# The routed gate product moved from VectorE to ScalarE and POOL in an attention and mixture-of-experts kernel

## Chip, cores and metric

One core of one Trainium2 chip. The metric is the device time of one execution in microseconds (us); three executions of the kernel before took 546.87, 548.35 and 548.81 us.

## What is computed

The input x has shape (4, 1024, 128). It is normalised over its last axis; xn goes to two branches, an attention and a mixture of experts, and the result is x + attention(xn) * silu(ffn(xn)). The expert branch, cut to what matters here (sixteen experts of inner size 64, four chosen per token, and a shared expert of inner size 128):

```python
hg = jnp.einsum('nh,eih->nei', xf, Wg)
hu = jnp.einsum('nh,eih->nei', xf, Wu)
act = jax.nn.silu(hg) * hu
y = jnp.einsum('nei,ne,ehi->nh', act, cw, Wd)          # cw: routing weight, 0 for experts not chosen
shared = jax.nn.silu(xf @ Ws_g.T) * (xf @ Ws_u.T) @ Ws_d.T
```

The attention has 16 heads of dimension 8, four over all earlier tokens and twelve over a window of 32.

## The kernel before

**Tiling.** Everything is kept transposed, with features on partitions and tokens on the free axis. A batch (1024 tokens) is two chunks of 512 columns. Two experts of inner size 64 fill 128 partitions, so a chunk has eight tiles t = 0 to 7 of two routed experts and a ninth, t = 8, for the shared expert: NUP = 9 tiles, EP = 8 of them routed, 72 in all over four batches and two chunks. All experts are computed for all tokens, and the routing weight, spread over the partitions of its expert by a matmul with pairsel (L749), multiplies the hidden values.

**One expert tile.** The silu is written as a product with 1 + tanh(g/2). The step ("up", c, t) makes up to three PSUM tiles on PE: the routing weight (L749), the gate product g and the up product u, each of the last two from three matmuls (L544 to L546). Then:

- ScalarE, step up: hid = tanh(0.5 g) (L828), and, for a routed tile, wrow = the routing row (L834).
- VectorE, step up: hid = (hid + 1) * g (L1121), which frees the gate's bank.
- VectorE, step times: hid = hid * u (through the helper tt, L933), which frees the up product's bank.
- POOL (GpSimd), step times, routed tiles only: hid = hid * wrow (L1243).
- PE, step down: the down projection accumulates in bank Y (L765). For a routed tile it waits for POOL, for the shared expert for VectorE.

hid has NHID = 5 buffers and wrow NWT = 3. PSUM's eight banks are a ring of three for the attention, a ring of three for the expert products and other preparations, one accumulator for the attention and one (Y) for the experts.

**The order of the work.** There is no scheduler at run time. Streams of steps are woven by strings written out by hand, one letter per step: R attention scores and products with the values, A making a head group's operands (strips, which is two DMAs from a plane in HBM, pads and kpads, which are the copies at L1065 and L1077, max, which is the row maxima at L1165 and L1167, maxdone, L1234, and qfull), X expert steps, P preparing the next batch, T its routing, V its values, C and 0 and 1 the context and output. FIRST_ORDER is the start, BODY_ORDER is a batch with the next batch's preparation woven in (three times), LAST_ORDER is the last batch. Every engine walks the same list of steps in this order and executes its own part of each, so an instruction that waits holds back everything later in the list on its engine, and only there.

Within the X stream the steps of a chunk follow each other so:

```python
for t in range(NUP + LAG_DOWN):          # LAG_DOWN = 3
    if 1 <= t <= NUP:
        out.append(("times", c, t - 1))
    if t < NUP:
        out.append(("up", c, t))
    if t >= LAG_DOWN:
        out.append(("down", c, t - LAG_DOWN))
```

The first six tiles of chunk 0 of a batch are computed in the section before it (SPLIT).

**Around it.** VectorE also makes the padded 16-bit operands by copies of 32 x 1024 elements within SBUF (L1065, L1077), the row maxima from PSUM, the routing (some forty small passes over 128 x 128 tiles in SBUF, mostly through L933), the layer norm and the reciprocals of the softmax sums (L1106). ScalarE evicts the scores through exp (L905) and the other PSUM tiles. POOL makes the diagonal of maxima (L1234), the low parts of x, q and k, and the context and output products.

## Time and profile before

| | |
|---|---|
| median of three runs | 548.35 us |
| profiled execution, own time | 548.62 us |
| its span | 546.8 us |
| PE busy | 482.4 us, 88% of the span |
| VectorE (DVE) busy | 435.4 us, 80%, 939 instructions |
| ScalarE (ACT) busy | 298.1 us, 55%, 582 instructions |
| POOL busy | 179.9 us, 33%, 167 instructions |
| mean granted TensorE clock | 0.982 of full speed |

The span is the stretch that the profiler's instruction records cover, and the execution's own time stands 1.8 us above it. Busy time counts an engine's instructions only, not its waits. PE is the matmul engine, PEld its weight loads, which overlap the matmuls. In a group of instructions, the idle time is that of the engine just before them, and the name behind it is what ended it. The chain of waits follows the work back from the last instruction, at each step to what released it or to the instruction before it on its engine.

### The profile page before, as it was taken

The page shows a single profiled execution, that of the slowest core. Times are in us where ns is not written, and L with a number is a line of the kernel's source. Part 1 is how long each engine was busy: PE and PEld are TensorE (multiplying, and loading weights), DVE is VectorE, ACT ScalarE, POOL GpSimd, SP SyncE. Part 2 cuts the span into 40 slices and gives each one's busy share as a digit, 9 for nine tenths or more (in the row PEclk, how much of TensorE's full clock was granted, in tenths as well). Part 3 has the DMA queues.
Part 4 walks back from the last instruction along what each step waited for, and adds up shares of the span by engine and source line. Part 5 has one row for each costly group of instructions (what it writes and reads, how often), then busy time and mean ns, then how long its engine had stood idle before and what let it go on. Part 6 is the DMA issues. An engine that isn't in the chain of part 4 may idle for free.

```text
span 546.8 us, 10352 instructions
## 1 busy us (share of the span) xinstructions
PE 482.4 (88%) x3832; PEld 286.5 (52%) x3832; DVE 435.4 (80%) x939; ACT 298.1 (55%) x582; POOL 179.9 (33%) x167
## 2 busy tenths in 40 slices
PE   1758978999999987999998997899999989989994
PEld 1546655555445754545445764545445656644442
DVE  6888798885998799876899789887799768788524
ACT  3524743656945453665955444564975445564862
POOL 3504621123524541113522633104341633103302
PEclk9969998999999999999999999999999999999997
DMA  8270210000310421000130331000040041000001
GB/s 209 87 222 0 79 40 1 2 2 1 115 40 2 115 78 41 2 1 0 54 102 1 91 104 40 1 2 1 1 155 1 26 130 40 2 0 2 1 0 38
DMA packets 26571, 25.00 MB, mean 46 GB/s; under 512 B 3462, under 2 KB 18842, under 8 KB 26522
## 3 DMA queue, kind: packets, MB, share of 16 engines
q1 hardware_dynamic: 26192, 24.06, 14.6%
q8 instruction: 30, 0.49, 0.4%
q10 hardware_dynamic: 330, 0.30, 0.3%
q14 instruction: 19, 0.16, 0.1%
HBM read 14.91 MB, written 9.44 MB: 45 GB/s over the span
## 4 chain that ended last, share of the span: by engine, by line
PE 43%; DVE 38%; issue 6%; ACT 4%; DVEq 4%; DMA 4%; POOL 1%; SPq 0%; POOLq 0%; ACTq 0%
PE bank L765 6%; DVE kpad L1077 5%; DVE qpad L1065 5%; PE bank L648 5%; DVE mxp L1167 5%; DVE denT L1106 4%; PE bank L544 4%; PE bank L546 3%; PE bank L545 3%; PE bank L725 3%; DVE mxp L1165 3%; DVE hid L933 3%; PE bank L709 3%; DMA kall<-planes 3%; PE bank L678 3%
## 5 line engine op out<-in xcount | busy, mean ns | idle before, releaser
L905 ACT ACTIVATE stage<-bank 128x512 f32<-128x512 f32 (+3 forms) x240 | 112.5, 519 | 68.6 <-PE bank L682 41.3
L1243 POOL TENSOR_TENSOR hid<-hid,wrow 128x512 f32<-128x512 f32 x64 | 82.6, 1293 | 150.6 <-DVE hid L933 150.5
L1165 DVE TENSOR_REDUCE mxp<-bank 128x1 f32<-128x512 f32 (+4 forms) x192 | 89.8, 518 | 13.6 <-PE bank L648 6.8
L1121 DVE SCALAR_TENSOR_TENSOR hid<-hid,bank 128x512 f32<-128x512 f32 x72 | 49.0, 680 | 40.7 <-ACT hid L828 40.5
L1234 POOL TENSOR_TENSOR maxd<-mxp,k 128x512 f16<-128x512 f32 x32 | 36.5, 1140 | 126.7 <-DVE mxp L1167 81.6
L765 PE MATMUL bank<-hid,down_w 128*128 128x512 f32 x144 | 76.0, 615 | 0.0
L828 ACT ACTIVATE hid<-bank 128x512 f32<-128x512 f32 x72 | 43.2, 600 | 45.7 <-PE bank L546 45.0
L544 PE MATMUL bank<-xh,up_hi 128*128 128x512 f32 x144 | 59.5, 413 | 4.7 <-DVE hid L933 3.1
L648 PE MATMUL bank<-kall,qpad 128*128 128x512 f16 (+4 forms) x192 | 50.1, 318 | 9.0 <-DVE mxp L1165 3.9
L546 PE MATMUL bank<-xl,up_hi 128*128 128x512 f32 x144 | 56.7, 394 | 0.0
L545 PE MATMUL bank<-xh,up_lo 128*128 128x512 f32 x144 | 56.5, 392 | 0.0
L678 PE MATMUL bank<-kpad,kall 128*128 128x512 f16 (+3 forms) x192 | 54.8, 330 | 1.6 <-ACT stage L905 0.9
L933 DVE TENSOR_TENSOR hid<-hid,bank 128x512 f32<-128x512 f32 x72 | 49.0, 680 | 1.3
L678 PEld LDWEIGHTS bank<-kpad,kall 128*128 128x128 f16 x192 | 17.4, 97 | 48.8 <-issue 31.1
L1065 DVE COPY qpad<-qtmp 32x1024 f16<-32x1024 f16 x64 | 35.5, 555 | 6.1 <-DMA kall<-planes 5.5
L709 PE MATMUL bank<-stage,vg 128*32 128x512 f32 (+3 forms) x384 | 40.0, 497 | 0.0
L834 ACT ACTIVATE wrow<-bank 128x512 f32<-128x512 f32 x64 | 38.2, 597 | 3.2 <-PE bank L749 3.2
L648 PEld LDWEIGHTS bank<-kall,qpad 128*128 128x128 f16 x192 | 17.3, 97 | 34.9 <-DVE mxp L1165 17.1
L898 ACT ACTIVATE qall<-bank 128x512 f16<-128x512 f32 x32 | 18.8, 597 | 28.7 <-PE bank L635 28.3
L544 PEld LDWEIGHTS bank<-xh,up_hi 128*128 128x128 f32 x144 | 27.2, 189 | 12.9 <-DVE hid L933 5.3
L1167 DVE TENSOR_REDUCE mxp<-bank 128x8 f32<-128x512 f32 x48 | 31.2, 685 | 2.5 <-PE bank L660 2.1
L749 PE MATMUL bank<-cwT,pairsel 128*128 128x512 f32 x64 | 32.9, 514 | 0.0
(158 smaller groups left out, 908.0 us busy)
## 6 DMA issues: line engine op xcount, KB each, us to landing
planes<-qkh SPq DMA_DIRECT2D x16, 256.0 KB, 3.5
qtmp<-planes SPq DMA_DIRECT2D x16, 256.0 KB, 2.6
kall<-planes SPq DMA_DIRECT2D x16, 256.0 KB, 3.0
xin<-in_L_attn_x_dram SPq DMA_DIRECT2D x4, 512.0 KB, 4.5
planes<-qkl SPq DMA_DIRECT2D x8, 256.0 KB, 3.5
xres<-in_L_attn_x_dram SPq DMA_DIRECT2D x4, 512.0 KB, 4.1
...
```

The source lines that it names most:

```text
L544: pe.matmul(ps[:], w_hi, x_hi, start=True, stop=False)
L545: pe.matmul(ps[:], w_lo, x_hi, start=False, stop=False)
L546: return pe.matmul(ps[:], w_hi, x_lo, start=False, stop=True)
L648: ins = pe.matmul(ps[:, 0:cols], qpad[:, j, :, :], kall[:, g % 2, CH * c:CH * c + cols], start=True, stop=not last, skip_group_check=True)
L678: ins = pe.matmul(ps[:, 0:cols], kall[:, g % 2, P * j:P * (j + 1)], kpad[:, g % 2, q0 // BLK:(q0 + cols) // BLK, h, :], start=True, stop=n ...
L765: pe.matmul(banks[Y][:], down_w[:, t, :], hid[:, i % NHID, :], start=(t == 0), stop=(t == NUP - 1)).then_inc(down_done, 1)
L905: act.activation(prob[:, t % NPROB, 0:cols], ps[:, 0:cols], ACT.Exp).then_inc(freed, 1)
L933: return dve.tensor_tensor(out_, a, b_, op)
L1065: ins = dve.tensor_copy(qpad[r, :, h, :], qtmp[r, g % 2, :].rearrange("p (j q) -> p j q", q=BLK))
L1165: ins = dve.tensor_reduce(mxp[:, c, j:j + 1], ps[:, 0:cols], AX_X, ALU.max)
L1167: ins = dve.tensor_reduce(mxp[:, 0, LOC * n:LOC * (n + 1)], ps[:].rearrange("p (j q) -> p j q", q=2 * BLK), AX_X, ALU.max)
L1243: pool.tensor_tensor(hid[:, i % NHID, :], hid[:, i % NHID, :], wrow[:, iw % NWT, :], ALU.mult)\
```

## The change

The product is taken in another grouping: before, ((tanh + 1) * g) * u * w, after, ((tanh + 1) * u) * (g * w). ScalarE copies the gate product from PSUM into a new SBUF tile, gates (one buffer), which frees the gate's bank. POOL multiplies the routing row in place with gates (step up, routed tiles), with a new semaphore, gated. VectorE makes one pass, hid = (hid + 1) * u (step times). POOL multiplies hid with that row, or, for the shared expert, with gates. PE's step down waits for POOL in every tile. Before filling gates for tile t, ScalarE waits for POOL's gating of tile t - 1, and for t = 0 for the shared expert's last multiplication of the chunk before. The three orders are woven anew.

```diff
--- before.py
+++ after.py
@@ -144,14 +144,14 @@
     return out
 
 
-FIRST_ORDER = ("PIPPIIPPPPITTPPPTTTPITTIIITIPIVIPIPPPPIPTPVXVXVXXIVXXVXXXIVXVXXVVXXX")
-BODY_ORDER = ("PAAXARXRXARRXAAAARARRRRAAAXAXAAPXRAARXRARARAAXXRRAAAAAAAAAARPRAAAXAAAXAARXAAAXXRRRARXAARARAARAAA"
-              "AARRRARAAARRRARAARAAXARRRXRARRAPAARXRRRARRXRAAARAXRRAXRRAXRRRAARAAPRRRPAARXRRXXRXRRRRRPRTPRRXRRR"
-              "RRPPTRRRXTRRTXXRRRRXCRRRCRPRRRRXXRRRRRRTXXPRXRTRRRRRRXPPPRRRRRPRRXRRRXRXRRTRXRRRXPRTTRP0CXCXV0PX"
-              "XVXX01VXVX1XX1VXXVXVVVVXX")
-LAST_ORDER = ("AXARARAXRXAAAAAAAAXRAAARRRRAAARAXRXRAAXXARXRAAAARRAAAAARARAAAXAAAXAAAXARARRRRRAXRRAAAARAAAXAARRX"
-              "RRAXRARRAAXRRRRAAAARAAARARAARARAAAXAARXRAXARAXRAARRXRXRRRRRRRRRRRAAXRRXRXRXRRXRRCRRRXCRRRRRRRRXR"
-              "RRRRRRRXXRRRRRRRRRRRRRRRXRRRRRRRRXRRRXRRRRRRXRRRRRRXRR0X0XCCXXXX0111")
+FIRST_ORDER = ("IPIIPPIPIPVTPIPPPPPTTTTITTIIVTVTIIVIXPXVIPPPXXPIXXVXXXVPPPXVXXVIVXXX")
+BODY_ORDER = ("PAAAXRXXARRRRXAARRAAAAARARXXAAAXPARAAARRRRAARAAXAAAXAARPAAARAAAXAAAXAAAXARRRRXAXAXRXAARRAAARRRAA"
+              "AAARARRAAARRRARARAAAXRARRXRARAPAARRXRARRRRRXAAARAXARRXXRARRRRAARRAAPRRPARXACRRXRXXRRRXRPRRTPRRRR"
+              "RRTPPRXRPRRRRXRXRXRRRRRTTXRRXXTRRRRRRTTXRXXRXRRRRRRPRCPRRRXRRPPRRRRRRRPXRRXRXRRRRRPTTRPCXCXV00XV"
+              "X11XVVV0XVXXVX1VXVPXXXVXX")
+LAST_ORDER = ("AAARRRXXAXAAAXRRAAARRRAAARXAAAAAXAAAXRXRARRAAAARRARAAAAAXRAAAXAAAXAAAXARRRARRAXRARRAAARAAAXAARRX"
+              "AAXRRRRARARRARRXAARAAAARARAARARAXAAARXARAAXARAAXRRRRRRXRRRRRRRRRAXAXRRXXRRXRXRRRRRRRRRRRRRXCXRRR"
+              "RRCRXRRRRRRRRRRXRRRRXRRRRRRRRRXRRRRRRRRRRXRXRRRRRRRRRXX0X0CCXXXX0111")
 
 
 FIRST_EXPERTS = expert_steps(0) + [("z", 0), ("z2", 0)]
@@ -389,6 +389,7 @@
         hid = sb("hid", [P, NHID, CH])
         wqk = hid[:, 0, 0:2 * D]
         wrow = sb("wrow", [P, NWT, CH])
+        gates = sb("gates", [P, CH])
         tz = sb("tz", [P, CH])
 
         filled = [sem(f"bank{i}_filled") for i in range(BANKS)]
@@ -431,6 +432,7 @@
         ctx_ready = sem("ctx_ready")
         hid_ready = sem("hid_ready")
         tanh_ready = sem("tanh_ready")
+        gated = sem("gated")
         o_ready = sem("o_ready")
         stored = [sem(f"stored{c}") for c in range(NCH)]
 
@@ -757,11 +759,7 @@
                         i = NUP * c + t
                         if t == 0:
                             fill(at, ("y", c))
-                        if t < EP:
-                            pe.wait_ge(hid_ready, of * NCH * EP + (EP * c + t + 1))
-                        else:
-                            up = ("up", c, t, "up")
-                            pe.wait_ge(emptied[at.bank(up)], at.taken(up))
+                        pe.wait_ge(hid_ready, of * NCH * NUP + (i + 1))
                         pe.matmul(banks[Y][:], down_w[:, t, :], hid[:, i % NHID, :],
                                   start=(t == 0), stop=(t == NUP - 1)).then_inc(down_done, 1)
                     elif kind == "outT":
@@ -826,11 +824,16 @@
                             act.wait_ge(down_done, of * NCH * NUP + (i - NHID + 1))
 
                         act.activation(hid[:, i % NHID, :], banks[at.bank(gate)][:], ACT.Tanh, scale=0.5).then_inc(tanh_ready, 1)
+                        if t > 0:
+                            act.wait_ge(gated, of * NCH * EP + (EP * c + t))
+                        elif of or c:
+                            act.wait_ge(hid_ready, of * NCH * NUP + NUP * c)
+                        act.activation(gates[:], banks[at.bank(gate)][:], ACT.Copy).then_inc(emptied[at.bank(gate)], 1)
                         if t < EP:
                             iw = EP * c + t
                             act.wait_ge(filled[at.bank(weight)], at.filled(weight))
                             if iw >= NWT:
-                                act.wait_ge(hid_ready, of * NCH * EP + (iw - NWT + 1))
+                                act.wait_ge(hid_ready, of * NCH * NUP + (NUP * ((iw - NWT) // EP) + (iw - NWT) % EP + 1))
                             act.activation(wrow[:, iw % NWT, :], banks[at.bank(weight)][:], ACT.Copy)\
                                 .then_inc(emptied[at.bank(weight)], 1)
                         continue
@@ -1114,20 +1117,14 @@
                         dve.wait_ge(tz_ready, at.of(s) * NCH + (c + 1))
                         dve.scalar_tensor_tensor(out=z[:, chunk(c)], in0=tz[:], scalar=1.0, in1=z[:, chunk(c)],
                                                  op0=ALU.add, op1=ALU.mult).then_inc(z2_ready, 1)
-                    elif kind == "up":
-                        i = NUP * s[1] + s[2]
-                        gate = s + ("gate",)
-                        dve.wait_ge(tanh_ready, at.of(s) * NCH * NUP + (i + 1))
-                        dve.scalar_tensor_tensor(out=hid[:, i % NHID, :], in0=hid[:, i % NHID, :], scalar=1.0,
-                                                 in1=banks[at.bank(gate)][:], op0=ALU.add, op1=ALU.mult)\
-                            .then_inc(emptied[at.bank(gate)], 1)
                     elif kind == "times":
                         c, t = s[1], s[2]
                         i = NUP * c + t
-                        gate, up = ("up", c, t, "gate"), ("up", c, t, "up")
-                        dve.wait_ge(emptied[at.bank(gate)], at.taken(gate))
+                        up = ("up", c, t, "up")
+                        dve.wait_ge(tanh_ready, at.of(s) * NCH * NUP + (i + 1))
                         dve.wait_ge(filled[at.bank(up)], at.filled(up))
-                        tt(hid[:, i % NHID, :], hid[:, i % NHID, :], banks[at.bank(up)][:], ALU.mult)\
+                        dve.scalar_tensor_tensor(out=hid[:, i % NHID, :], in0=hid[:, i % NHID, :], scalar=1.0,
+                                                 in1=banks[at.bank(up)][:], op0=ALU.add, op1=ALU.mult)\
                             .then_inc(emptied[at.bank(up)], 1)
                     elif kind == "weights" and s[1] == 2:
                         continue
@@ -1234,13 +1231,22 @@
                         pool.tensor_tensor(maxd[:, blocks, :], mxp[:, 0, blocks].unsqueeze(2).broadcast_to([P, BPC, BLK]),
                                            const32("eye32").unsqueeze(1).broadcast_to([P, BPC, BLK]), ALU.mult)\
                             .then_inc(maxd_ready, 1)
-                    elif kind == "times" and s[2] < EP:
+                    elif kind == "up" and s[2] < EP:
+                        gate, weight = s + ("gate",), s + ("weight",)
+                        row = wrow[:, (EP * s[1] + s[2]) % NWT, :]
+                        pool.wait_ge(emptied[at.bank(gate)], at.taken(gate))
+                        pool.wait_ge(emptied[at.bank(weight)], at.taken(weight))
+                        pool.tensor_tensor(row, row, gates[:], ALU.mult).then_inc(gated, 1)
+                    elif kind == "times":
                         c, t = s[1], s[2]
-                        up, weight = ("up", c, t, "up"), ("up", c, t, "weight")
-                        i, iw = NUP * c + t, EP * c + t
-                        pool.wait_ge(emptied[at.bank(weight)], at.taken(weight))
+                        gate, up = ("up", c, t, "gate"), ("up", c, t, "up")
+                        i = NUP * c + t
+                        pool.wait_ge(emptied[at.bank(gate)], at.taken(gate))
                         pool.wait_ge(emptied[at.bank(up)], at.taken(up))
-                        pool.tensor_tensor(hid[:, i % NHID, :], hid[:, i % NHID, :], wrow[:, iw % NWT, :], ALU.mult)\
+                        if t < EP:
+                            pool.wait_ge(gated, at.of(s) * NCH * EP + (EP * c + t + 1))
+                        pool.tensor_tensor(hid[:, i % NHID, :], hid[:, i % NHID, :],
+                                           wrow[:, (EP * c + t) % NWT, :] if t < EP else gates[:], ALU.mult)\
                             .then_inc(hid_ready, 1)
                     elif kind == "ctx":
                         q = CH * s[1] + QTR * s[2]
```

## Rows read from the trace of the kernel before

**Rows 1.** The page's table of busy time by engine.

```profile
PE 482.4 (88%) x3832; PEld 286.5 (52%) x3832; DVE 435.4 (80%) x939; ACT 298.1 (55%) x582; POOL 179.9 (33%) x167
```

**Rows 2.** Windows by batch: length; busy PE, PEld, DVE, ACT, POOL; clock, DMA.

```profile
0.00:62.90 62.90, 39.75 (x200) 30.49 (x201) 51.03 (x136) 27.42 (x49) 23.15 (x34) 0.92 0.41 113
...
190.90:317.00 126.10, 117.10 (x952) 69.00 (x951) 107.13 (x231) 71.88 (x142) 43.87 (x38) 1.00 0.14 43
...
443.50:546.80 103.30, 89.69 (x784) 48.01 (x782) 65.92 (x119) 55.32 (x111) 24.89 (x23) 0.97 0.07 21
```

**Rows 3.** The page's chain of waits, shares by engine.

```profile
PE 43%; DVE 38%; issue 6%; ACT 4%; DVEq 4%; DMA 4%; POOL 1%; SPq 0%; POOLq 0%; ACTq 0%
```

**Rows 4.** Windows through the second body, columns as in rows 2.

```profile
190.90:227.00 36.10, 31.36 (x399) 19.83 (x397) 33.74 (x77) 18.14 (x33) 10.37 (x9) 1.00 0.14 45
...
254.00:281.10 27.10, 26.94 (x126) 13.57 (x126) 20.72 (x53) 22.55 (x43) 11.80 (x11) 1.00 0.25 78
281.10:299.00 17.90, 16.07 (x126) 8.46 (x124) 16.58 (x29) 9.55 (x23) 3.25 (x4) 1.00 0.01 1
299.00:317.00 18.00, 17.48 (x79) 12.66 (x80) 14.02 (x30) 7.20 (x15) 11.52 (x10) 1.00 0.30 87
```

**Rows 5.** Groups by line: operations of an expert tile (busy, mean, idle before).

```profile
L1243 POOL TENSOR_TENSOR hid<-hid,wrow 128x512 f32<-128x512 f32 x64 | 82.6, 1293 | 150.6 <-DVE hid L933 150.5
...
L1121 DVE SCALAR_TENSOR_TENSOR hid<-hid,bank 128x512 f32<-128x512 f32 x72 | 49.0, 680 | 40.7 <-ACT hid L828 40.5
L933 DVE TENSOR_TENSOR hid<-hid,bank 128x512 f32<-128x512 f32 x72 | 49.0, 680 | 1.3
```

**Rows 6.** DVE's timeline: the instruction after an L1121 pass.

```profile
208.22 0.68 DVE L1121 SCALAR_TENSOR_TENSOR hid<-hid,bank 128x512 f32<-128x512 f32 x1
208.82 1.28 DVE L1167 TENSOR_REDUCE mxp<-bank 128x8 f32<-128x512 f32 x2
```

**Rows 7.** The 16-bit copies: groups by line, then shortest, median and longest.

```profile
L1065 DVE COPY qpad<-qtmp 32x1024 f16<-32x1024 f16 x64 | 35.5, 555 | 6.1 <-DMA kall<-planes 5.5
...
L1077 DVE COPY kpad<-kall 32x1024 f16<-32x1024 f16 x48 | 29.2, 608 | 0.5
...
L1065 DVE COPY qpad<-qtmp x64: 405/420/1420, 37.6 to 466.7; 32x1024 f16<-32x1024 f16 x64
...
L1077 DVE COPY kpad<-kall x48: 404/423/1178, 41.6 to 461.8; 32x1024 f16<-32x1024 f16 x48
```

**Rows 8.** Small routing passes: groups, then DVE's and POOL's timelines.

```profile
L933 DVE TENSOR_TENSOR cmp<-cmp 128x128 f32<-128x128 f32 x8 | 6.6, 825 | 0.6
...
L933 DVE TENSOR_TENSOR msk<-msk,gm 128x128 f32<-128x128 f32 x4 | 3.9, 978 | 0.3
...
L933 DVE TENSOR_TENSOR eq<-msk,top 128x128 f32<-128x128 f32 x4 | 3.3, 821 | 0.0
L933 DVE TENSOR_TENSOR cmp<-cmp,k 128x128 f32<-128x128 f32 x4 | 3.2, 793 | 0.3
...
264.48 1.17 DVE L933 TENSOR_TENSOR cmp<-cmp 128x128 f32<-128x128 f32 x1
...
267.38 0.29 DVE L933 TENSOR_TENSOR cmp<-cmp 128x128 f32<-128x128 f32 x1
...
264.34 1.16 POOL L1224 TENSOR_TENSOR qkl<-sT,qkh 128x512 f16<-128x512 f32 x1 [3.46 <-ACT qkh L893]
```

**Rows 9.** ScalarE's timeline: a tanh and the row copy behind it.

```profile
271.09 0.64 ACT L828 ACTIVATE hid<-bank 128x512 f32<-128x512 f32 x1
271.57 0.66 ACT L834 ACTIVATE wrow<-bank 128x512 f32<-128x512 f32 x1
```

**Rows 10.** Timelines of POOL and ScalarE, then the chain, before a body's end.

```profile
302.10 1.06 POOL L1234 TENSOR_TENSOR maxd<-mxp,k 128x512 f16<-128x512 f32 x1
...
315.99 1.09 ACT L898 ACTIVATE qall<-bank 128x512 f16<-128x512 f32 x2 [2.87 <-PE bank L635]
...
317.05 4.29 DMA kall<-planes
```

## The prediction

> **What bounds the kernel now.** I read the page's table of busy times first [rows 1]. TensorE is busy 88% of the span and VectorE 80%; ScalarE (55%) and POOL (33%) have room. The windows by batch then show that the kernel is a start of 62.9 us, three bodies of some 126 us and a last batch of 103.3 us, and that in a body PE is busy 117.10 and DVE 107.13 of 126.10 us [rows 2]. The end of a matmul is modelled in this trace, so a busy PE need not be a full one. The chain of waits says how the two share the limit: 43% of the chain is PE, 38% DVE, 4% ACT, 1% POOL [rows 3]. Inside a body the bound changes [rows 4]: in the first 36.1 us (maxima and paddings of the local heads) DVE is busy 33.74 us, in the middle (254.0 to 281.1) PE is busy 26.94 of 27.10 and DVE 20.72, from 281.1 to 299.0 DVE again with 16.58 of 17.90, and in the last 18 us (six expert tiles packed together) PE with 17.48, while POOL, idle elsewhere, is busy 11.52. The groups of lines give the price of an expert tile [rows 5]: two DVE passes of 680 ns (L1121 and the hid group of L933), a POOL pass of 1293 ns. DVE also stands idle 40.7 us in front of L1121, waiting for the tanh.
>
> **DVE, removed.** 72 passes go, one per tile. In a full DVE queue the next instruction starts 0.60 us after such a pass (208.22, then 208.82 [rows 6]), so the pass costs 0.60 us of queue, not 0.68: 72 x 0.60 = 43.2 us. The idle time in front of L1121 shrinks too, since the one pass that is left stands where the second stood, steps behind the tanh. I count that at nothing: it lies mostly where PE is the fuller engine, and PE's work covers it.
>
> **POOL, added.** A gating pass for each of 64 tiles, and a pass for the 8 shared-expert tiles that had none: 72 x 1.293 = 93.1 us on 179.9. Their own room is there; their neighbour is the question. The four copies into the padded operands have medians of 420 and 423 ns but means of 555 and 608, with a maximum of 1420 [rows 7]. The excess, 64 x 0.135 + 48 x 0.185 = 17.5 us, falls on copies beside a POOL pass. The routing's small passes show the same [rows 8]: a 128x128 cmp takes 0.29 us at 267.38, with POOL at rest, and 1.17 us at 264.48, with a POOL pass running since 264.34. By that 0.29, the groups cmp, msk, eq and cmp with the constant hold 8 x 0.535 + 4 x (0.688 + 0.531 + 0.503) = 11.2 us more. Together 28.7 us of DVE time for 167 POOL instructions, 0.17 us each. For 72 more passes I take the same mean: 72 x 0.172 = 12.4 us given back to DVE. The bounds are nothing (every new pass beside a DVE pass that reads PSUM) and 72 x 1.0 us, the longest excess of a copy (1.42 less 0.42).
>
> The Trainium skill (SBUF — State Buffer, Who interferes with whom) says that GpSimd and a DVE instruction with two SBUF inputs or in a two-port mode exclude each other for a whole instruction, whoever issues second waiting; by it all 72 passes could each stop DVE for their full length, and DVE's queue would grow. Direction and kind of victim agree with the rows; how often it happens is the rows' to say.
>
> **Sum on DVE.** 43.2 - 12.4 = 30.8 us, 7.1% of its 435.4 us. DVE's part of the chain is 0.38 x 546.8 = 207.8 us; shrunk alike, it gives **-14.7 us**.
>
> **ACT, added.** 72 copies of the gate product. A copy right behind another ACT pass costs its start-to-start 0.48 us (271.09, then 271.57 [rows 9]): 34.6 us, 11.6% of 298.1. On ACT's 4% of the chain (21.9 us) that is **+2.5 us**. The copy also frees the gate's bank, which until now waited for DVE's first pass; PE was seldom held by it, so nothing is counted.
>
> **POOL's part of the chain.** 1% is 5.5 us; 51.7% more work there is **+2.8 us**.
>
> **The added waits.** There is one gates buffer. ACT may fill it for tile t+1 only after POOL's gating of tile t, and on POOL that gating stands behind the final multiplication of tile t-1, which waits for DVE. Behind ACT's wait stand the row copy of the same tile and every exp and eviction after it. A tight loop is gate copy, row copy, gating: 0.48 + 0.66 + 1.29 = 2.4 us [rows 5, 9], and POOL's two passes are 2.6 us a tile. The packed stretch now takes 18.0 us for six tiles, 3.0 each, so it fits, barely. PE's multiplication for the shared expert now waits for POOL instead of DVE, 1.29 us later, eight times; the two steps of lag behind it cover that.
>
> **The orders.** The three interleavings move many steps within one pattern; the number of every kind of instruction stays, the DMAs included (strips issue two each, q and k three each). In the body, the strips of head group 0 go ahead of six exp steps, two parts of the routing and an expert tile, on SP past nothing else; their data are wanted later than now, so I count nothing. In the start, a memset of the padded keys goes ahead of the statistics and three weight tiles go ahead of most of the routing: DVE has 11.9 us idle there [rows 2], so this could give or take a few us. I count nothing, and the range has room for it. The late maximum of group 0 (maxdone) moves behind three more tiles on POOL. Today that pass starts at 302.10, while the ACT pass that depends on it runs at 315.99 [rows 10], and the strips of group 1, on the chain at 317.05 as the DMA into kall, wait for that. Those 13 us cover a move; if the cover is gone, each of three bodies starts up to two POOL passes late, 3 x 2.6 = 7.8 us. What is late next, when DVE is shorter, is PE.
>
> **Total.** -14.7 + 2.5 + 2.8 = -9.4 us, from the profiled execution's 548.62 us (a span of 546.8 and 1.8 around it) to 539.2. That execution stands 0.3 us above the median of the three runs, 548.35, so the number is **539.0 us**.
>
> **Rivals.**
> 1. *The bound is PE, and DVE's relief only makes DVE idle.* For it: PE's 117.10 of 126.10 us, against DVE's 107.13 [rows 2]; a body could gain at most those 9 us of PE idle time. Against: 38% of the chain. Then only the start, with six tiles, gains 6 x 0.60 x 0.38 = 1.4 us: 547 us. Chance 0.18.
> 2. *The larger gain.* The new POOL passes meet no copies and the handoffs are hidden: 43.2 / 435.4 x 207.8 = 20.6 us, 528 us. For it: the heaviest copying lies outside the packed expert tiles. Against: the collisions now, and PE's small room. Chance 0.17.
> 3. *Slower: POOL passes hold DVE at the paddings and the routing.* In the DVE-bound stretch the passes for tiles 6 to 8 run beside 16-bit copies that already grow from 0.42 to 1.42 us. Break-even is where DVE's saving, times 207.8/435.4, equals the 5.3 us of the other engines: 43.2 - 72e = 11.1, e = 0.45 us per added pass; today's mean is 0.17, the worst 1.0. At 0.72, DVE grows by 8.6 us, the chain by 4.1, with the 5.3 9.4 us: 558 us; at 1.0 it is 568. Chance 0.15. The page named above is this rival's rule: at 1.29 us a pass DVE grows by 49.9 us, and the time would be 578.
>
> The forecast itself, 534 to 545 us, has 0.50. The 80% range is 528 to 552 us: it takes in rival 1, half of rival 2 down to its full value, and rival 3 up to just under its middle. A measurement can tell about 0.5% from no change, 2.7 us. Faster by more: 0.50 + 0.17 = 0.67; within: 0.18; slower: 0.15.
>
> **What would show it.** In the profile of the changed kernel: DVE busy near 400 us, with 72 fewer passes; ACT near 335, POOL near 273. The means of the copies at L1065 and L1077 tell the collisions: near 0.65 us for the forecast, near 0.58 as now for rival 2, 0.85 or more for rival 3. DVE's share of the chain should fall and PE's rise; body lengths should be 123 to 124.5 us. Waits of the ACT gate copy for POOL above some 10 us in total would speak for the single buffer as the price I underrated; bodies of 126 us with DVE idle behind PE would speak for rival 1. The prediction is wrong in kind if the copies keep their means and the time still does not fall.

## The result, and the profile after

The change made the kernel slower: 580.66 us (median of four runs, 580.32 to 582.14) against 548.53 for the kernel before beside it, a ratio of 1.060 with a 95% interval of 1.057 to 1.064. The forecast was 539.0 us, the range ended at 552. The profiled execution took 580.32 us, its span is 578.5.

The page's table of busy times, its row of the granted clock over 40 slices, and the chain's shares by engine (they answer to [rows 1] and [rows 3]; the clock's row is in tenths of full speed):

```profile
PE 491.5 (85%) x3832; PEld 289.9 (50%) x3832; DVE 428.7 (74%) x867; ACT 331.1 (57%) x654; POOL 272.4 (47%) x239
...
PEclk9869998898989999999997999889998999999999
...
PE 42%; DVE 36%; ACT 7%; issue 7%; DVEq 4%; DMA 2%; POOL 1%; SPq 0%; POOLq 0%; ACTq 0%
```

The 72 DVE passes are gone (939 instructions became 867), 43.2 us of queue at the 0.60 us from start to start of [rows 6], yet DVE's busy time fell by 6.7 us only: what is left grew by 36.5 us. PE ran the same 3832 instructions and was busy 9.1 us longer. The groups of lines say which passes grew (they answer to [rows 5] and [rows 7]; the new line L1239 is the gating pass):

```profile
L1248 POOL TENSOR_TENSOR hid<-hid,wrow 128x512 f32<-128x512 f32 x64 | 83.3, 1302 | 16.8 <-DVE hid L1126 9.9 <-POOL wrow L1239 6.8 <-DVE mxp L1164 0.2
L1239 POOL TENSOR_TENSOR wrow<-wrow,gates 128x512 f32<-128x512 f32 x64 | 82.8, 1294 | 105.5 <-ACT wrow L837 105.3
...
L1126 DVE SCALAR_TENSOR_TENSOR hid<-hid,bank 128x512 f32<-128x512 f32 x72 | 48.7, 677 | 39.4 <-ACT hid L826 19.8 <-PE bank L548 19.1
L1068 DVE COPY qpad<-qtmp 32x1024 f16<-32x1024 f16 x64 | 45.1, 705 | 9.7 <-DMA kall<-planes 8.9
L831 ACT ACTIVATE gates<-bank 128x512 f32<-128x512 f32 x72 | 42.9, 596 | 3.9 <-POOL wrow L1239 3.9
L1080 DVE COPY kpad<-kall 32x1024 f16<-32x1024 f16 x48 | 33.5, 699 | 0.6
```

The pass that is left, with one input in SBUF and one in PSUM, is as long as before (677 ns against 680). The copies within SBUF went from 555 to 705 and from 608 to 699 ns, 14 us together, and the third kind (L1087, L1084 before) adds 2.8. Most of the rest lies in small passes within SBUF for the routing and the layer norm: eight over 128 x 64 elements (pm from sfc) went from 1.5 to 6.4 us in total, four that make sc from 0.9 to 3.9. ScalarE's copy waited for POOL 3.9 us in all, so little speaks for the single buffer as the price (no run changes it).

The windows by batch (columns as in [rows 2], with boundaries at the next batch's first layer-norm statistics), start, three bodies, last batch:

```profile
0.00:62.45 62.45, 37.97 (x195) 28.67 (x196) 49.01 (x124) 29.07 (x53) 27.19 (x32) 0.89 0.41 113
62.45:201.96 139.51, 122.40 (x951) 71.77 (x950) 107.00 (x213) 80.42 (x160) 67.91 (x61) 0.95 0.12 37
201.96:336.38 134.42, 119.43 (x952) 70.14 (x950) 105.32 (x213) 80.03 (x159) 67.06 (x56) 0.97 0.13 40
336.38:474.30 137.92, 121.38 (x954) 70.85 (x951) 105.98 (x213) 80.66 (x161) 68.07 (x57) 0.96 0.12 38
474.30:578.50 104.20, 90.29 (x786) 48.49 (x786) 61.36 (x107) 60.87 (x123) 42.20 (x36) 0.99 0.07 21
```

With the same boundaries the kernel before has 61.80, 127.83, 126.10, 126.44 and 104.63 us. All of the loss is in the bodies: 11.7, 8.3 and 11.5 us. The windows of the second body, cut at four events, say where. Stretch 1 runs from the statistics to the first copy of L1084 (L1087 after), which is the local heads with the paddings; stretch 2 to the tanh of the router's scores; stretch 3 is the routing, up to the pass that writes cw; stretch 4 runs to the next statistics and ends with most of the packed tiles. The kernel before:

```profile
189.63:227.89 38.26, 33.52 (x429) 21.49 (x428) 35.01 (x84) 19.98 (x35) 12.21 (x10) 1.00 0.13 43
227.89:254.64 26.75, 24.97 (x213) 14.25 (x207) 22.07 (x45) 13.61 (x30) 6.78 (x7) 1.00 0.01 1
254.64:290.06 35.42, 34.43 (x192) 16.58 (x196) 29.12 (x70) 25.74 (x53) 13.59 (x12) 1.00 0.19 61
290.06:315.73 25.67, 24.18 (x134) 16.69 (x131) 20.93 (x34) 12.55 (x24) 11.29 (x10) 1.00 0.21 61
```

And the kernel after:

```profile
201.96:242.47 40.51, 33.76 (x441) 22.15 (x438) 36.18 (x80) 21.20 (x39) 17.80 (x15) 1.00 0.15 47
242.47:270.03 27.56, 24.64 (x200) 13.93 (x197) 21.78 (x42) 15.04 (x32) 12.16 (x11) 1.00 0.01 2
270.03:300.77 30.74, 29.16 (x136) 13.87 (x134) 21.55 (x52) 25.82 (x51) 16.64 (x14) 1.00 0.22 69
300.77:336.38 35.61, 31.86 (x182) 20.19 (x183) 25.81 (x39) 17.96 (x38) 20.45 (x18) 0.90 0.13 37
```

Stretch 1 has four DVE passes fewer and DVE is busier, 36.18 against 35.01 us: the saving is given back within it. Stretch 4 has a clock of 0.90, where before has 1.00. Stretches 3 and 4 can only be compared as a sum, 66.4 against 61.1 us, since the new orders move PE's work over the boundary (x192 and x134 became x136 and x182). The orders thus had to be taken apart from the instructions first.

### The profile page after: what moved, and what is told of

Its sections match the earlier page's. It is cut to its first block, busy times and chain, and to the rows that moved or that the text cites. A ratio compares the mean times of both kernels' runs of the same rounds, so it can differ in the third digit from the quotient of the medians.

```text
span 578.5 us, 10499 instructions
## 1 busy us (share of the span) xinstructions
PE 491.5 (85%) x3832; PEld 289.9 (50%) x3832; DVE 428.7 (74%) x867; ACT 331.1 (57%) x654; POOL 272.4 (47%) x239
## 4 chain that ended last, share of the span: by engine, by line
PE 42%; DVE 36%; ACT 7%; issue 7%; DVEq 4%; DMA 2%; POOL 1%; SPq 0%; POOLq 0%; ACTq 0%
DVE qpad L1068 6%; PE bank L763 6%; PE bank L650 5%; DVE kpad L1080 5%; DVE mxp L1164 4%; DVE mxp L1162 4%; PE bank L546 4%; PE bank L548 3%; PE bank L547 3%; PE bank L711 3%; PE bank L680 3%; DMA kall<-planes 2%; DVE hid L1126 2%; ACT stage L908 2%; DVE xin L939 2%
## 5 line engine op out<-in xcount | busy, mean ns | idle before, releaser
L908 ACT ACTIVATE stage<-bank 128x512 f32<-128x512 f32 (+3 forms) x240 | 112.4, 523 | 78.2 <-PE bank L684 46.6
L1239 POOL TENSOR_TENSOR wrow<-wrow,gates 128x512 f32<-128x512 f32 x64 | 82.8, 1294 | 105.5 <-ACT wrow L837 105.3
L763 PE MATMUL bank<-hid,down_w 128*128 128x512 f32 x144 | 79.4, 640 | 0.0
L1231 POOL TENSOR_TENSOR maxd<-mxp,k 128x512 f16<-128x512 f32 x32 | 36.6, 1142 | 84.3 <-DVE mxp L1164 49.0
L650 PE MATMUL bank<-kall,qpad 128*128 128x512 f16 (+4 forms) x192 | 52.8, 331 | 13.6 <-DVE mxp L1162 10.3
L680 PE MATMUL bank<-kpad,kall 128*128 128x512 f16 (+3 forms) x192 | 58.2, 343 | 1.1 <-DVE mxp L1162 0.6
L1068 DVE COPY qpad<-qtmp 32x1024 f16<-32x1024 f16 x64 | 45.1, 705 | 9.7 <-DMA kall<-planes 8.9
L831 ACT ACTIVATE gates<-bank 128x512 f32<-128x512 f32 x72 | 42.9, 596 | 3.9 <-POOL wrow L1239 3.9
L711 PE MATMUL bank<-stage,vg 128*32 128x512 f32 (+3 forms) x384 | 41.1, 509 | 0.0
L656 PE MATMUL bank<-kbf 128*128 128x512 bf16 x48 | 19.4, 404 | 21.9 <-DVE qpad L1068 21.9
```

The costliest lines, as they stand in the source:

```text
L650: ins = pe.matmul(ps[:, 0:cols], qpad[:, j, :, :], kall[:, g % 2, CH * c:CH * c + cols], start=True, stop=not last, skip_group_check=True)
L680: ins = pe.matmul(ps[:, 0:cols], kall[:, g % 2, P * j:P * (j + 1)], kpad[:, g % 2, q0 // BLK:(q0 + cols) // BLK, h, :], start=True, stop=n ...
L763: pe.matmul(banks[Y][:], down_w[:, t, :], hid[:, i % NHID, :], start=(t == 0), stop=(t == NUP - 1)).then_inc(down_done, 1)
L908: act.activation(prob[:, t % NPROB, 0:cols], ps[:, 0:cols], ACT.Exp).then_inc(freed, 1)
L1068: ins = dve.tensor_copy(qpad[r, :, h, :], qtmp[r, g % 2, :].rearrange("p (j q) -> p j q", q=BLK))
L1239: pool.tensor_tensor(row, row, gates[:], ALU.mult).then_inc(gated, 1)
```

## The experiments

Three theories. **A: POOL's passes hold DVE** by traffic in SBUF (the prediction's third rival). **B: POOL's queue.** The passes of the experts stand ahead of others that PE waits for, the maxima's above all (L1231, before L1234), whoever else is at work. **C: the orders**, which I had counted as nothing, or the added waits.

### Instructions and orders apart

e1_old_orders has the instructions of after in the orders of before, e2_new_orders the reverse.

```diff
 e1_old_orders, on the kernel after:
-BODY_ORDER = ("PAAAXRXXARRRRXAARR...
+BODY_ORDER = ("PAAXARXRXARRXAAAAR...
 e2_new_orders, on the kernel before:
-BODY_ORDER = ("PAAXARXRXARRXAAAAR...
+BODY_ORDER = ("PAAAXRXXARRRRXAARR...
 (FIRST_ORDER and LAST_ORDER likewise)
```

> The changed kernel's instructions, woven in the three orders of the kernel before. Theory P (the 72 added POOL passes cost: they stop DVE's SBUF copies and routing passes, and they pace the packed expert tiles): the time stays near the changed kernel's, 575 to 590 us, with DVE's copies still at means of 0.65 us or more. Theory O (the new orders are what lost the time, by work put late): back to 540 to 552 us. Theory W (the single gates buffer and the longer chain from POOL to ScalarE): 570 to 590 us too, but with the ScalarE gate copy waiting for POOL for 20 us or more in total.

> The kernel before's instructions, woven in the new orders. Theory P: the orders are nearly neutral, 545 to 556 us. Theory O: most of the 32 us comes with the orders alone, 570 us or more. Theory W says the same as P here: 545 to 556 us.

e1: 583.51 us, ratio 1.064 (1.060 to 1.068). e2: 583.4 us, 1.065 (1.062 to 1.068). Two things follow. The instructions alone cost 35 us. And the new orders are far from neutral: on the old work they cost 35 us as well (DVE waits 80.0 us for the tanh where it waited 40.5, and PE 18.8 us for the paddings where it waited 5.1), and on the new work they neither cost nor bring more than 3 us. They belong to the new instructions, and neither order makes those fast. Everything below that asks for the mechanism can use the old orders, where the stretches hold the same work. The windows of e1's second body by stretch, then stretch 1 of its third body:

```profile
202.36:244.58 42.22, 33.48 (x429) 21.46 (x428) 34.89 (x80) 21.73 (x39) 17.86 (x14) 1.00 0.13 39
244.58:271.38 26.80, 24.92 (x213) 14.15 (x207) 20.40 (x42) 15.00 (x32) 10.15 (x9) 1.00 0.01 2
271.38:306.78 35.40, 34.57 (x196) 16.70 (x196) 30.75 (x65) 27.82 (x58) 20.23 (x17) 1.00 0.19 60
306.78:334.84 28.06, 24.90 (x130) 16.37 (x123) 17.35 (x28) 15.39 (x30) 18.78 (x16) 1.00 0.20 55
334.84:382.05 47.21, 37.82 (x429) 24.65 (x428) 34.92 (x80) 21.74 (x39) 17.84 (x14) 0.89 0.12 36
```

Against before: +4.0, +0.1, 0.0, +2.4 us. In the two middle stretches PE is busy 93 to 98% of the time, and DVE's busy time is 1.7 us less in one and 1.6 us more in the other without effect. Stretch 1 loses though DVE is busy no more than before, and the second body is the mildest: in the first and the third, with the same instructions, stretch 1 takes 47.8 and 47.2 us, both at a clock of 0.89. I come back to that. PE's waits for the maxima's pass of POOL are 20.1 us in all of e1, 8.1 before; in after they are 7.0, but there PE waits 21.9 us for the paddings, 5.1 before (9.9 in e1). So the two orders pay at different places. In stretch 4 POOL, with two passes of 1.29 us a tile and its others, is the one that the packed tiles wait for.

### Is it the added passes?

e3_short_gating takes the kernel after and lets the gating pass work on 32 of 512 columns.

```diff
-pool.tensor_tensor(row, row, gates[:], ALU.mult).then_inc(gated, 1)
+pool.tensor_tensor(row[:, 0:32], row[:, 0:32], gates[:, 0:32], ALU.mult).then_inc(gated, 1)
```

> The changed kernel with POOL's gating pass cut to 32 of 512 columns, every wait and semaphore kept; the routing row is multiplied with the gate product in those columns only, so the output lacks the gate factor in the rest. Theory P: the gating passes' own length is the cost; with 64 of the 72 added passes shortened from 1.29 to some 0.2 us the time falls below the kernel before, 530 to 550 us. Theory W: the waits stay, so most of the loss stays, 565 us or more. Theory O: also 565 us or more.

560.1 us, 1.021 (1.019 to 1.024): 20.6 us less than after. POOL is busy 66.2 us less and DVE 26.2 us less (402.5). Every instruction and wait of the change is there, so two thirds of the loss is the length of the 64 gating passes. I had expected 530 to 550 us if it were all of it: 12 us over the kernel before are left, and no run divides them among ScalarE's copies, the shared expert's passes and the orders.

e4_before_plus_passes goes the other way: the kernel before, with 64 POOL passes on which nothing depends. They stand where the gating stands; they read one column of a constant, broadcast, and write 128 x 512.

```diff
+elif kind == "up" and s[2] < EP:
+    pool.wait_ge(emptied[at.bank(weight)], at.taken(weight))
+    held = half[:, 0:1].broadcast_to([P, CH])
+    pool.wait_ge(idled, at.of(s) * NCH * EP + EP * s[1] + s[2])
+    pool.tensor_tensor(idle_out[:], held, held, ALU.mult).then_inc(idled, 1)
 (idle_out and idled are a new tile and a new semaphore)
```

> The kernel before, its own orders, with one POOL pass of 128x512 fp32 added for each of the 64 routed tiles at the step up; it reads and writes tiles that nobody else uses, so nobody waits for its result, it only takes POOL's time and its way to SBUF. Theory P: DVE loses some 0.5 us or more a pass as in the changed kernel, and has not lost the 72 passes of its own: 575 to 600 us. Theory W or O: nothing depends on the passes and POOL has room, 547 to 553 us.

578.31 us, 1.052 (1.047 to 1.057). Nothing waits for these passes, no DVE pass is removed, and the time is 30 us longer. The page's busy times and the group of the passes:

```profile
PE 494.7 (86%) x3832; PEld 295.6 (51%) x3832; DVE 447.8 (78%) x939; ACT 298.8 (52%) x582; POOL 244.8 (42%) x231
...
L1244 POOL TENSOR_TENSOR idle_out<-half 128x512 f32<-128x512 f32 x64 | 67.4, 1053 | 119.7 <-ACT wrow L836 119.5
```

DVE grew by 12.4 us, exactly what the forecast had given back to it (0.19 us a pass here, 0.17 there). By the forecast's own rates that is 12.4 x 207.8/435.4 + 67.4/179.9 x 5.5 = 8 us. It cost 30. This run judges the pricing alone, apart from how many collisions there are.

e5_passes_off_sbuf keeps the passes and takes the traffic away: a power on 5 columns, which lasts as long.

```diff
-pool.tensor_tensor(idle_out[:], held, held, ALU.mult).then_inc(idled, 1)
+pool.tensor_tensor(idle_out[:, 0:5], idle_out[:, 8:13], half[:, 0:5], ALU.pow).then_inc(idled, 1)
 (and a memset of idle_out at the start)
```

> The kernel before with 64 added POOL instructions as in e4, at the same steps and behind the same wait, but each a pow over 5 columns: about as long, with next to no traffic to SBUF. Theory P1 (the added passes cost by shutting VectorE's copies and two-input passes out of SBUF): back to 548 to 556 us. Theory P2 (they cost by holding POOL's queue, by their length and by their wait, so that its other passes come late): stays at 568 to 580 us. In between, both.

566.87 us, 1.033 (1.030 to 1.036). Its passes have a mean of 1177 ns, 12% longer than e4's, and DVE's busy time is 436.5 us, 1.1 above before. So 18 us come nearly without collisions, by occupying POOL's queue (B) and what the clock adds to it, and the other 12 of e4's 30 by traffic (A); since e5's passes are longer, that is traffic's least share. Neither theory alone stands. The trace of e5 has the queue at work, and the clock beside it. For 28 us the second body's stretch 1 keeps PE's times of the kernel before. Then a phase at the lower clock (0.57 in the window 222 to 226) puts it 1.6 us behind, though PE's instructions and waits up to there were the same. Then the last maxima's pass starts at 232.78, directly behind an added pass, and PE stands idle 1.43 us before the matmul that needs it (at 233.93; in the kernel before 0.13 us, at 226.63): that is the queue's 1.3 us. By stretches of the second body, stretch 3, with the routing's small passes, takes 39.2 us in e4 and 35.4 in e5, as before; stretch 1 takes 43.2 and 41.1, stretch 4 27.3 and 29.4. This division is rough, because the clock falls in other places in other bodies: in the first and third body of e5 stretch 3 takes 36.9 and 37.1 us, and its stretch 4 takes 29.4 at a clock of 0.94 and 27.7 in the first body at 1.00.

e9_wait_only leaves e4's wait and drops the pass.

```diff
 pool.wait_ge(emptied[at.bank(weight)], at.taken(weight))
-held = half[:, 0:1].broadcast_to([P, CH])
-pool.wait_ge(idled, at.of(s) * NCH * EP + EP * s[1] + s[2])
-pool.tensor_tensor(idle_out[:], held, held, ALU.mult).then_inc(idled, 1)
```

> The kernel before with POOL's wait for ScalarE's row copy at the step up (64 times), as in e4 and e5, and no pass behind it. e5 left 18 us that are not traffic: if the wait's place is that cost (it holds the maxima's passes that stand behind it), 558 to 567 us; if the length of the passes is, 548 to 551 us.

548.6 us, 1.000 (0.998 to 1.003). The wait costs nothing; the occupation does. Two more runs move the gating pass from the step up to the step times, so that POOL never stands waiting for it ahead of others: e10_late_gating_old_orders on e1, e11_late_gating on after.

```diff
-elif kind == "up" and s[2] < EP:
-    ...
-    pool.tensor_tensor(row, row, gates[:], ALU.mult).then_inc(gated, 1)
 elif kind == "times":
     ...
+    if t < EP:
+        pool.tensor_tensor(row, row, gates[:], ALU.mult).then_inc(gated, 1)
```

> e1 (the changed kernel's instructions in the old orders, 583.5 us) with POOL's gating pass moved from the step up to the step times, right ahead of the final multiplication, so that its wait for ScalarE no longer stands ahead of the maxima. If the held queue costs: 565 to 576 us. If the passes' length and traffic cost: 580 to 586 us.

> The changed kernel in its own orders with the same move of the gating pass. The new orders already put the maxima's pass of head group 3 ahead of the first tile of chunk 1, so the hold should be small here: 576 to 582 us. Below 573 us would say that the hold is the price in these orders too; above 584 us that the pass is better done early.

583.44 us, 1.063 (1.058 to 1.068), as e1; and 586.38 us, 1.069 (1.065 to 1.073), 6 us above after: there the pass is better done early. The theory that POOL's early wait holds its queue fell with these and e9.

### Where the passes hurt

e6_packed_passes has e4's passes only for the six packed tiles of each batch (24), e7_other_passes only for the others (40).

```diff
 e6_packed_passes:
-elif kind == "up" and s[2] < EP:
+elif kind == "up" and s[1] == 0 and s[2] < SPLIT_PAIR:
 e7_other_passes:
-elif kind == "up" and s[2] < EP:
+elif kind == "up" and s[2] < EP and not (s[1] == 0 and s[2] < SPLIT_PAIR):
 (the count of idled in the wait likewise)
```

> As e4, with the added passes only at the six tiles of each batch that are packed together (24 of the 64). P1: the copies next to them are the only ones hit, 552 to 558 us. P2, POOL pacing the packed tiles: 560 to 568 us, a body's last stretch some 3 to 4 us longer. If neither: 548 to 551 us.

> As e4, with the added passes only at the other ten routed tiles of each batch (40 of the 64). P1: 560 to 570 us, since the paddings of the local heads stand beside them. P2: 555 to 565 us, by the maxima's pass held behind the wait of the added pass. With e6 it should add up to e4's 30 us; a sum well below that would speak for a cost that needs both, as POOL's backlog running into the paddings.

555.27 us, 1.012 (1.009 to 1.015), and 567.58 us, 1.035 (1.032 to 1.038): 6 and 19 us, 25 together against e4's 30. Per pass 0.3 and 0.5 us. In the second body of e7 stretch 1 grows by 5.1 us and stretch 3 by 3.8 (in the first body by 1.9 and 2.2): the places with copies, maxima and routing are the dearer ones.

e12_shared_only isolates one place: the kernel before with the change for the 8 shared-expert tiles only. Each of these loses a DVE pass and gains a ScalarE copy and a POOL pass, which was not there before.

```diff
 DVE, step up:
+if s[2] == EP:
+    continue
 POOL:
+elif kind == "times" and s[2] == EP:
+    ...
+    pool.tensor_tensor(hid[:, i % NHID, :], hid[:, i % NHID, :], gates[:], ALU.mult).then_inc(hid_ready, 1)
 (ScalarE's copy, DVE's step times and PE's wait for these tiles as in the change)
```

> The kernel before, its own orders, with the change made for the shared expert's tiles only (8 of 72: ScalarE copies the gate, VectorE makes one pass, POOL multiplies by the gate, no gating pass). By the prediction's way of counting, 1 to 2 us faster than the kernel before. By the changed kernel's mean price for a tile (32 us over 72) 3 to 4 us slower. If only the gating pass makes the trouble, within 1.5 us of the kernel before or faster.

557.63 us, 1.016 (1.013 to 1.020). Eight passes cost 9 us, more than one each, and far more than any of my three expectations. Stretch 1 of its second body grew from 38.3 to 41.5 us; in the first and the third body it grew by 0.8 and 3.7 us. These three make up 7.7 us, as much as the profiled execution's span grew (554.5 against 546.8); the other stretches of the second body kept their length within 0.3. The timelines of DVE, POOL and PE there (start, length, instruction, and in brackets the idle time before it):

```profile
213.62 0.69 DVE L1134 SCALAR_TENSOR_TENSOR hid<-hid,bank 128x512 f32<-128x512 f32 x1
214.22 3.44 DVE L1066 COPY qpad<-qtmp 32x1024 f16<-32x1024 f16 x4
...
214.45 1.30 POOL L1253 TENSOR_TENSOR hid<-hid,gates 128x512 f32<-128x512 f32 x1 [3.33 <-DVE hid L1134]
215.72 1.22 POOL L1244 TENSOR_TENSOR maxd<-mxp,k 128x512 f16<-128x512 f32 x1
...
217.00 0.61 PE L635 MATMUL bank<-qtmp,k 128*128 128x512 f16 x1 [2.89 <-POOL maxd L1244]
```

The same instructions in the kernel before, timelines of DVE, POOL and PE:

```profile
214.44 2.06 DVE L1065 COPY qpad<-qtmp 32x1024 f16<-32x1024 f16 x4
...
213.88 1.05 POOL L1234 TENSOR_TENSOR maxd<-mxp,k 128x512 f16<-128x512 f32 x1 [2.55 <-DVE mxp L1167]
...
214.98 0.39 PE L634 MATMUL bank<-qtmp,k 128*128 128x512 f16 x1 [0.66 <-POOL maxd L1234]
```

Read it line by line. DVE's pass on hid ends and releases POOL, so POOL's pass starts beside DVE's next instructions, of necessity. Those are the four padding copies, 3.44 us beside this pass and the next, in place of 2.06 beside the maxima's pass alone. Behind that POOL pass stands the maxima's pass, which before ran first and now starts 1.8 us later. PE, which needs it, waits 2.89 us in place of 0.66. And its next matmul takes 0.61 us in place of 0.39. The windows of e12, the wait, the 7 us behind it, and the next 7, say why (the clock is the third figure from the end):

```profile
214.00:217.00 3.00, 0.11 (x2) 0.01 (x1) 2.97 (x4) 0.60 (x1) 2.49 (x2) 0.96 0.00 0
217.00:224.00 7.00, 6.44 (x58) 4.22 (x58) 3.75 (x14) 2.94 (x5) 0.00 (x0) 0.53 0.01 2
224.00:231.00 7.00, 6.73 (x64) 3.91 (x61) 6.51 (x12) 3.85 (x7) 1.50 (x2) 1.00 0.00 1
```

PE stood idle for 2.9 us, and the granted clock was 0.53 for the next 7 us, nearly all at the lower of the two levels (1.2 GHz), before it was back at full. Of the 3.3 us that this stretch 1 grew by, 2.4 are PE's busy time (35.90 us for the work that took 33.52). One DVE pass traded for one POOL pass thus cost collision, queue and clock at once. That PE's idle time is what lowers the clock is stated by the Trainium skill (TensorE: Matmul & The Clock Gate, HAM oscillation — how this bites in real kernels), and this row agrees in direction; that the length of a wait alone does not decide it is shown in the last section.

e14_shared_moved tests this scene: e12 with the shared tile's step times moved by a few steps, so that the maxima's pass and the copies are issued first.

```diff
+def moved(steps, step, behind):
+    steps.remove(step)
+    steps.insert(steps.index(behind) + 1, step)
+    return steps
 ...
-return woven(LAST_ORDER, streams)
+return moved(woven(LAST_ORDER, streams), ("times", 0, 8), ("pads", 3))
 (BODY_ORDER likewise)
```

> e12 (the change for the shared expert alone, 557.6 us) with one step of the orders moved in the bodies and the last batch: the product with the up tile of the shared expert of chunk 0 stands behind the padding of head group 3 instead of ahead of the second half of group 2's maxima. POOL's new pass then no longer stands ahead of the maxima's pass that PE waits for, and no longer runs beside the padding's copies. If these two are the price that e12 paid: 546 to 551 us. If the price is elsewhere (ScalarE's copy, the down projection's wait for POOL): 555 us or more.

548.3 us, 0.999 (0.997 to 1.001): all 9 us are back, by one step. The timelines of POOL and DVE:

```profile
212.45 1.27 POOL L1250 TENSOR_TENSOR maxd<-mxp,k 128x512 f16<-128x512 f32 x1 [2.55 <-DVE mxp L1183]
215.73 1.27 POOL L1259 TENSOR_TENSOR hid<-hid,gates 128x512 f32<-128x512 f32 x1 [2.01 <-DVE hid L1140]
...
212.40 2.47 DVE L1072 COPY qpad<-qtmp 32x1024 f16<-32x1024 f16 x4
214.90 0.69 DVE L1140 SCALAR_TENSOR_TENSOR hid<-hid,bank 128x512 f32<-128x512 f32 x1
215.50 1.05 DVE L1181 TENSOR_REDUCE mxp<-bank 128x1 f32<-128x32 f32 x5
```

The pass on hid now has row maxima behind it, which read PSUM: they take 1.05 us beside a POOL pass, against 1.06 without one. The eight DVE passes saved bring nothing, though. e18_before_moved is the control, the same move in the kernel before.

> Control of e14: the kernel before with that one step moved and nothing else. If the move is neutral here: 547 to 550 us, and e14's equality with the kernel before means that the change for the shared expert is worth nothing. Below 546 us would mean that the move itself gains and that the change costs what it gains.

548.49 us, 1.001 (0.999 to 1.003). The move has no value of its own; it only takes away what the change had put there. e16_old_orders_moved is e1, the change on all the tiles, with the same move.

> e1 (the whole change in the old orders, 583.5 us) with the one step moved as in e14. The same two troubles lie in it, but four other POOL passes stand in the same stretch (two tiles, two passes each) and POOL paces the packed tiles. If e14's 9 us is there to be had: 573 to 577 us. If the other passes hold the maxima and the paddings anyway: 580 us or more.

574.91 us, 1.050 (1.044 to 1.056), 8.6 us below e1: about as much comes back as in e14, and 27 us of loss are left. One of a batch's 18 tiles is mended, the others are not.

### The relief by itself

e17_short_dve_pass asks what DVE's relief is worth when nothing is added: the kernel before, with L1121 on 32 of 512 columns.

```diff
-dve.scalar_tensor_tensor(out=hid[:, i % NHID, :], in0=hid[:, i % NHID, :], scalar=1.0,
-                         in1=banks[at.bank(gate)][:], op0=ALU.add, op1=ALU.mult)
+dve.scalar_tensor_tensor(out=hid[:, i % NHID, 0:32], in0=hid[:, i % NHID, 0:32], scalar=1.0,
+                         in1=banks[at.bank(gate)][:, 0:32], op0=ALU.add, op1=ALU.mult)
```

> The kernel before with VectorE's first pass of each tile (L1121, the one that the change removes) cut to 32 of 512 columns, every wait kept and nothing added anywhere: the worth of the relief by itself. The factor 1 + tanh times the gate is left out in the other columns. The prediction's sum (DVE's saving times DVE's share of the chain) says some 36 us of DVE queue, 17 us of time: 529 to 534 us. If PE holds the time wherever DVE is relieved: 543 to 549 us.

542.87 us against 547.93, 0.990 (0.986 to 0.994). The chain's shares, and the four stretches of the second body:

```profile
PE 56%; DVE 28%; issue 4%; DMA 4%; ACT 3%; DVEq 3%; POOL 1%; SPq 0%; POOLq 0%; ACTq 0%
...
186.16:223.75 37.59, 32.94 (x424) 21.52 (x428) 33.02 (x85) 19.98 (x35) 12.97 (x10) 1.00 0.14 44
223.75:250.53 26.78, 24.90 (x212) 14.20 (x208) 20.61 (x45) 13.63 (x30) 6.31 (x6) 1.00 0.01 1
250.53:284.93 34.40, 33.98 (x191) 16.68 (x196) 27.50 (x69) 25.64 (x53) 13.55 (x12) 1.00 0.19 62
284.93:309.96 25.03, 23.97 (x133) 16.72 (x131) 18.28 (x33) 12.56 (x24) 11.30 (x10) 1.00 0.22 62
```

DVE is busy 31.0 us less, as much as the forecast's sum on DVE (30.8), and the time falls by 5.1 us, where the sum said 14.7. The second body gives 2.3 us: 0.7, 1.0 and 0.6 in stretches 1, 3 and 4. Even stretch 3, where PE is busy 97% of the time before, gains. The chain's share passed from DVE (38 to 28%) to PE (43 to 56%): the work on it had another way to the end at nearly the same time.

### The clock

The third body of e1 has a stretch 1 of 47.2 us where the second has 42.2. e13_filled_waits is e1 with six useless matmuls (their result is overwritten) ahead of six of PE's waits in each batch.

```diff
+if (g, c) in ((1, 1), (2, 1), (3, 0)):
+    for _ in range(6):
+        pe.matmul(ps[:], constbf("identb"), constbf("win"), start=True, stop=True, skip_group_check=True)
 pe.wait_ge(maxd_ready, b * HG * NCH + (g * NCH + c + 1))
 ...
 (the same six, for g = 1 to 3, ahead of the wait for qpad_ready)
```

> e1 (the changed kernel's instructions in the old orders, 583.5 us) with six matmuls of 128x512 bf16 whose results are overwritten, put on PE ahead of six waits of each batch in the local heads' stretch (maxima's pass of POOL for groups 1 to 3, padded queries of groups 1 to 3), 1.3 us each at full clock. They do no useful work. If PE's granted clock, which in e1 stands at half for 10.5 us of that stretch in the first and third body after PE idle times of 2.9 us, is a price of its own: no such half-clock stretches, and 572 to 579 us in spite of the added work. If the clock only follows the stalls and costs nothing: 583 to 592 us.

582.84 us, 1.062 (1.059 to 1.065); the expected gain (572 to 579 us) did not come. Stretch 1 of the second and the third body:

```profile
199.80:242.71 42.91, 40.02 (x457) 24.88 (x464) 34.88 (x80) 21.65 (x39) 18.03 (x14) 1.00 0.12 39
...
333.42:376.26 42.84, 40.05 (x457) 24.88 (x464) 34.87 (x81) 21.64 (x39) 17.84 (x14) 1.00 0.11 39
```

The third body's stretch fell from 47.2 to 42.8 us with the clock at 1.00: 4.4 us was the price of a clock of 0.89 there, or a little more, since the fillers take time as well. Over the whole execution the first body fell by 2.8 us and the third by 4.7, but the last batch grew from 107.8 to 112.4 us and the second body by 1.1, so that most of the gain was given back. They are a way to see the clock's price and not, placed like this, a way to save it.

### Two moves in the new orders

The prediction named one move as a possible price: the late maxdone, which in the new body order stands behind three more tiles. e8_maxdone_early puts it back. The windows of after showed another that I had not named: the paddings of head group 0 stand directly ahead of its maxima, with a PE wait of 3.9 us on them and a clock of 0.50 in the 6 us behind. e15_pads_early puts those paddings 11 steps earlier. The windows of after (the wait, then the stretch behind it):

```profile
301.00:304.00 3.00, 0.00 (x0) 0.00 (x0) 2.96 (x6) 0.00 (x0) 1.31 (x1) 0.89 0.00 0
304.00:310.00 6.00, 5.68 (x34) 2.57 (x34) 3.88 (x6) 1.15 (x3) 1.29 (x2) 0.50 0.00 0
310.00:313.00 3.00, 3.00 (x40) 1.46 (x37) 2.39 (x4) 1.41 (x5) 0.59 (x1) 0.97 0.03 5
```

```diff
 e8_maxdone_early, BODY_ORDER:
-"...RRRPTTRPCXCXV00XV" "X11XVVV0XVXXVX1VXVPXXXVXX"
+"...RRRPTTRPCXCXV00PX" "VX11XVVV0XVXXVX1VXVXXXVXX"
 e15_pads_early, BODY_ORDER (the P of the paddings):
-"...RRRRTTXRXXRXRRRRRRPRCPRRR..."
+"...RRRRTTXPRXXRXRRRRRRRCPRRR..."
```

> The changed kernel with one move undone: the late maximum of head group 0 stands again before the second packed tile (in the three bodies), not before the last but one. If the cover of that move is gone, as the prediction's bound had it, the time falls by 3 to 8 us; if POOL's backlog is the same wherever that pass stands, it moves less than 2 us either way.

> The changed kernel with one step of BODY_ORDER moved: the padding of head group 0 stands 11 steps earlier, right behind the products of the shared expert of chunk 1, as in the orders before. In the changed kernel PE waits 3.9 us for its copies once a body and then runs 7 us at half clock. If that move was a part of the loss: 568 to 576 us. If DVE is simply full there and the wait only moves: 578 us or more.

e8: 582.54 us (576.41 to 586.53; the median without its slowest run is 581.29), ratio 1.058 (1.052 to 1.065): no gain, though a few us either way would not show over such a spread. e15: 576.4 us, 1.052 (1.048 to 1.056), 4.3 us below after, just outside the 568 to 576 expected. No price shows for the move that I feared, and one that I had not looked at cost 4 us.

## Why the prediction was wrong

**The bound, right in its parts.** Stretches 2 and 3 are nearly PE's: in e1's second body they keep 26.8 and 35.4 us, but stretch 3 gains 1.0 us in e17 and loses 3.8 in e4. In stretch 1 PE and DVE take turns.

**DVE, removed: right in size.** 72 passes of 0.60 us of queue; behind the one that is left the next instruction still starts 0.60 us later.

**DVE's saving turned into time: the sum was too large.** "Sum on DVE" shrank DVE's part of the chain in proportion and got -14.7 us. e17 gives DVE the same relief, with no cost beside it, and gains 5.1 us. A share of the chain is what could be gained if nothing else were close behind; PE was. (Its short passes still take 0.18 us each; 36.0 of the group's 49.0 us are gone.) Rival 1 had this mechanism. It gave the relief 1.4 us, too little, and had no loss in it.

**POOL, added: the step that failed.** "1% is 5.5 us; 51.7% more work there is +2.8 us." e4 shows the price of occupying POOL with nothing depending on it: 64 passes of 1.05 us cost 30 us, of which 18 remain when they hardly touch SBUF (e5). As I read it, POOL had 1% of the chain because its few passes in PE's way met a free queue. The share told how little they waited and not how much they would, with a 1.29 us pass in front of them. After the change the share is still 1%: what shows is PE's waiting for DVE's paddings, 21.9 us in place of 5.1. In e1, whose packed tiles POOL sets, it is 11%.

**The give-back: undersized.** I took today's mean of 0.17 us per POOL instruction, over all of them. It is 36.5 us, 0.51 for each of 72 passes, above the 0.45 that rival 3 named as its break-even (e1, in the old orders: 43.2 less 15.2 is 28.0 us, 0.39 a pass, and as slow). Most of it belongs to the gating passes: with these short (e3), DVE is busy 26.2 us less, 0.41 for each of 64. Why a new pass costs more than an old one is not shown for them; they are released by ScalarE's row copy. The shared expert's eight are released by a DVE pass and so meet DVE's next instruction every time; in e12 that was the padding copies, where I had placed rival 3. It had the mechanism and its place. Its 558 us at 0.72 missed what lies around the collision: the queue, and the clock. The Trainium skill's rule (SBUF — State Buffer, Who interferes with whom), weighed in the prediction, agrees with the victims: copies within SBUF grow, the pass with one SBUF input and the row maxima don't. What the prediction made of it, every pass a full collision, was nearer than my forecast in the time it gave (578 us), but by a sum that the trace does not bear out: DVE's busy time fell, by 6.7 us.

**The clock: no term at all.** The mean granted clock fell from 0.982 to 0.960. Time at the lower level, as 2 x (1 - clock) x span, is 19.7 us before and 46.3 after. PE's busy time for the same 3832 instructions rose by 9.1 us, and that is the most direct size of this term. On PE's old work the same shows: PE is busy 12.3 us more in e4, which lost 30, 7.0 more in e5, which lost 18, and 4.5 more in e12, which lost 9.

**ACT, added; the waits.** ScalarE grew by 33.0 us where I counted 34.6, with 7% of the chain. The single buffer, which I had called barely enough, cost ScalarE 3.9 us of waiting (7.5 in e1). Where POOL's two passes a tile do set the time, in stretch 4, it is 2.4 us a body (e1), at full clock.

**The orders: counted as nothing, by an argument about each move.** e2 refutes this in general (the same moves cost 35 us on the old work) and e15 in one place.

**The signs to look for.** I had named a mean of the copies of 0.85 us as the sign of rival 3; they reached 0.70, and the time was slower still. DVE near 400 us was wrong (428.7), POOL near 273 and ACT near 335 right (272.4 and 331.1). DVE's share of the chain did fall, to 36%, but PE's did not rise (42%), and no body came near 124 us.

What stays open: how after's 32 us divide among collisions, queue and clock, since they occur in the same places and each brings on the next; what ScalarE's copies cost by themselves, since no run adds only them (e4, which has none, already costs 30 of e1's 35 us); why the new orders cost the old work 35 us beyond the late tanh and paddings; and whether an order exists in which the new instructions win. The relief alone gives the scale: in the old orders e17 gained 5 us with 36.0 of 49.0 us taken off, in proportion some 7 for the whole pass (an estimate), and the version that changes the shared tiles only, with the scene mended (e14), only equals the kernel before. No kernel that does all the work was faster than that one.
